# First halves in steps of four chunks, and GpSimd adding to the running total

## The reference

```
def _propagate(all_emb, rows, cols, vals):
    acc = all_emb
    x = all_emb
    for _ in range(N_LAYERS):
        x = jax.ops.segment_sum(vals[:, None] * x[cols], rows, num_segments=N_NODES)
        acc = acc + x
    return acc / (N_LAYERS + 1)
...
users_emb = all_users[users] + _upsample_nearest(mm_users[users])
items_emb = all_items + _upsample_nearest(mm_items)
rating = users_emb @ items_emb.T
rating = rating + bias_user[users] + bias_item.T
return jax.nn.sigmoid(rating)
```

## Time and profile before

| | us |
|---|---|
| median of 3 runs | 5386.34 (5384.41 to 5394.33) |
| the profiled execution | 5386.6 |
| its span | 5384.8 |
| VectorE busy | 4793.2 (89%) |
| TensorE busy | 3361.2 (62%) |
| ScalarE busy | 2443.1 (45%) |
| GpSimd busy | 2415.1 (45%) |

### The profile page before, as it was taken

One profiled execution on the slowest core, in us unless ns is written; L12 is line 12 of the kernel. 1 busy time (PEld: TensorE's weight loads), 2 busy tenths in 40 slices (PEclk: granted clock), 3 DMA queues, 4 the chain that ended last, 5 costly groups with the idle time before them and its releaser, 6 DMA issues.

```text
span 5384.8 us, 195868 instructions
## 1 busy us (share of the span) xinstructions
PE 3361.2 (62%) x71235; PEld 2864.2 (53%) x71473; DVE 4793.2 (89%) x7569; ACT 2443.1 (45%) x4368; POOL 2415.1 (45%) x2161
## 2 busy tenths in 40 slices
PE   5600021111288888777678888867768888867767
PEld 4500011110277777666567777756657777766652
DVE  9989999999999999877799999967789999977778
ACT  0035555553366666500156666620046666640027
POOL 0038763330177777700067777730037777760000
PEclk9955555555699999999999999989989999989989
DMA  9960000300188778799968878889968777879999
GB/s 329 415 260 0 0 0 3 5 0 0 64 248 253 248 246 247 234 321 328 279 213 251 248 256 249 249 276 328 328 191 255 249 245 246 249 241 328 328 281 357
DMA packets 840272, 1191.20 MB, mean 221 GB/s; under 512 B 150792, under 2 KB 667583, under 8 KB 839825
## 3 DMA queue, kind: packets, MB, share of 16 engines
q1 hardware_dynamic: 716032, 816.66, 53.2%
q0 software_dynamic: 123872, 372.78, 18.0%
q10 hardware_dynamic: 304, 1.00, 0.1%
HBM read 638.35 MB, written 551.90 MB: 221 GB/s over the span
## 4 chain that ended last, share of the span: by engine, by line
DVE 28%; DMA 28%; issue 20%; POOL 9%; PE 6%; ACT 5%; SPq 1%; DVEq 1%; POOLq 0%; another core or an unknown queue 0%; ACTq 0%
DMA ring<-posts 15%; DMA posts<-ring 9%; POOL posts L775 9%; DVE store L1064 6%; PE psum L1501 4%; DVE total L861 3%; ACT new L695 3%; DVE store L1042 3%; DVE ring L1271 3%; DVE store L1043 2%; DMA out<-new 2%; DVE new L1243 2%; DVE ring L1256 2%; DVE ring L1295 2%; DMA ring<-lanes_d 1%
## 5 line engine op out<-in xcount | busy, mean ns | idle before, releaser
L775 POOL DMA_INDIRECT posts<-ring x1884 | 1852.6, 983 | 1740.6 <-DVE ring L1256 1154.0
L1477 PE MATMUL psum<-store,ring 128*128 x45216 | 2086.2, 197 | 497.9 <-DVE ring L1271 461.6
L1477 PEld LDWEIGHTS psum<-store,ring 128*128 128x128 bf16 x45216 | 1815.1, 100 | 769.2 <-issue 591.4
L695 ACT ACTIVATE new<-new 128x512 bf16<-128x512 uint8 x1884 | 1067.8, 614 | 0.0
L1271 DVE TENSOR_SCALAR ring<-ring,lane_f 128x1024 bf16<-128x1024 bf16 x1884 | 959.7, 551 | 23.4 <-DMA ring<-lanes_d 22.0
L1295 DVE TENSOR_TENSOR ring<-ring,wide_lane 128x1024 bf16<-128x1024 bf16 x948 | 612.9, 688 | 300.1 <-ACT ring L705 300.1
L1256 DVE TENSOR_TENSOR ring<-new 128x1024 bf16<-128x1024 bf16 x942 | 652.2, 692 | 93.8 <-ACT new L695 63.3
L693 ACT ACTIVATE ring<-new 128x512 bf16<-128x512 bf16 x942 | 585.9, 622 | 310.3 <-DVE new L1243 308.2
L750 POOL TENSOR_TENSOR ring<-store 128x1024 f32<-128x1024 f32 x157 | 369.6, 2354 | 660.6 <-DVE store L982 306.3
L1243 DVE TENSOR_TENSOR new<-psum,vals_m 128x512 f32<-128x512 f32 x942 | 644.1, 684 | 6.1 <-PE psum L1477 4.0
L1501 PE MATMUL psum<-ring 128*128 128x64 bf16 x11520 | 387.4, 193 | 188.7 <-DVE ring L1295 180.9
(11 more groups left out here) (228 smaller groups left out, 2666.1 us busy)
## 6 DMA issues: line engine op xcount, KB each, us to landing
ring<-lanes_d SPq DMA_DIRECT2D x471, 512.0 KB
ring<-posts SPq DMA_DIRECT2D x240, 772.0 KB, 6.7
store<-posts SPq DMA_DIRECT2D x234, 772.0 KB, 6.7
posts<-store SPq DMA_DIRECT2D x2, 30880.0 KB, 166.7
posts<-store SPq DMA_DIRECT2D x2, 30108.0 KB, 128.5
out<-new SPq DMA_DIRECT2D x96, 500.0 KB, 8.4
posts<-ring POOLq DMA_INDIRECT x1884
store<-L_rec_bias_item SPq DMA_DIRECT2D x1, 3125.0 KB, 13.8
```

Source lines behind the costliest of these rows:

```text
L695: last = nc.scalar.activation(digits[s][:, k, :], scaled_byte[s][k], ACT.Copy, scale=scale)
L775: pool.indirect_dma_start(out=posts[:, :], out_offset=bass.IndirectOffsetOnAxis(ap=dring[:, h, c:c + 1], axis=0), in_=msg[:, n, :], in_off ...
L1477: last = pe.matmul(psum[:, d % 4, (n % 2 * BLOCK + b) * F:(n % 2 * BLOCK + b + 1) * F], of, xflat[:, bass.ds(at_d[c] * F + (k * XT + x * F ...
```

## The change

A step of the first half becomes four chunks (157 steps a layer): each of VectorE's and ScalarE's instructions on it is twice as long, and there are half as many. The scale now stands between a step's two one-hots. The message ring is refilled by quarters of four slots, each with a semaphore of its own. GpSimd waits for a message and adds to `s_pace` once for four scatters. The additions to the running total (and the copies in layer 0) move from VectorE to GpSimd, ahead of a layer's scatters; whatever overwrites `new` waits for as many of them as it needs (`TAKEN_FOR`, two, four and seven). So that this works the one-hots, digits and powers move into `new`, the scaled sums into `ring`, and `rest` to another place in `ring`. SyncE's first loads of a layer wait only until the second half before them has been read. `WAYS` is 2, as before, and the loop at the end of the second half (`ADD_BODIES`) is written in another way with the same instructions.

```diff
-        hot = [ring[:, 2048 + s * 1024:3072 + s * 1024].bitcast(BF16).rearrange("p (k e) -> p k e", k=2) for s in range(2)]
+        hot = [new[:, s * WAYS * 1024:(s + 1) * WAYS * 1024].bitcast(BF16).rearrange("p (k e) -> p k e", k=WAYS) for s in range(2)]
...
-        scaled = [new[:, s * 512:(s + 1) * 512] for s in range(2)]
+        dring = ring[:, 10336:10352].bitcast(I32).rearrange("p (h e) -> p h e", h=4)
+        scaled = [ring[:, 2048 + s * 1024:3072 + s * 1024] for s in range(2)]
...
-        digits = [new[:, 1024 + s * 512:1536 + s * 512].bitcast(BF16).rearrange("p (k e) -> p k e", k=2) for s in range(2)]
-        power = [new[:, 2048 + s * 256:2304 + s * 256].bitcast(BF16) for s in range(2)]
+        digits = [new[:, 6144 + s * 1024:7168 + s * 1024].bitcast(BF16).rearrange("p (k e) -> p k e", k=2) for s in range(2)]
+        power = [new[:, 8192 + s * 512:8704 + s * 512].bitcast(BF16) for s in range(2)]
...
-        rest = [ring[:, s * SPLIT * F:(s + 1) * SPLIT * F].rearrange("p (t f) -> p t f", f=F) for s in range(2)]
+        rest = [ring[:, 5200 + s * SPLIT * F:5200 + (s + 1) * SPLIT * F].rearrange("p (t f) -> p t f", f=F) for s in range(2)]
...
-                sp.wait_ge(s_x3, (layer + 1) * SPLITS)
-                def lanes(i, h, n):
-                    for b in range(n // 4):
-                        sp.wait_ge(s_hots, i * 8 + (layer * DUOS + h * 4 + b * 2 + 2))
+                if layer:
+                    sp.wait_ge(s_unit, layer * ITERS + GOTS)
...
-                def refill(i, h, first, n):
+                def refill(i, h, first):
 
                     if layer or not first:
-                        act.wait_ge(s_scat[h], i * 128 + layer * SENT_ROWS[h])
-                    at = bass.ds(i * 16 + h * 8, n)
-                    nc.scalar.activation(dring[:, h, 0:n], dest_m[:, at], ACT.Copy)
-                    nc.scalar.activation(msg_lanes[:, h * 16:h * 16 + 2 * n, :], lanes_m[:, at, :].rearrange("p s (a e) -> p (s a) e", e=2), ACT.Copy)
-
-                def take_apart(i, first, pairs=8):
-                    for d in range(pairs):
+                        act.wait_ge(s_scat[h], i * 64 + layer * SENT_ROWS[h])
+                    at = bass.ds(i * 16 + h * 4, 4)
+                    nc.scalar.activation(dring[:, h, :], dest_m[:, at], ACT.Copy)
+                    nc.scalar.activation(msg_lanes[:, h * 8:h * 8 + 8, :], lanes_m[:, at, :].rearrange("p s (a e) -> p (s a) e", e=2), ACT.Copy)
+
+                def take_apart(i, first, quads=4):
+                    for d in range(quads):
                         s = d % 2
-                        if d % 4 == 0:
-                            refill(i, d // 4, first, min(8, 2 * pairs - 2 * d))
-                        act.wait_ge(s_scaled, i * 8 + (layer * DUOS + d + 5))
-                        nc.scalar.activation(msg_parts[:, 0, 4 * d:4 * d + 4, :], scaled_high[s], ACT.Copy).then_inc(s_high, 1)
+                        refill(i, d, first)
+                        act.wait_ge(s_scaled, i * 4 + (layer * QUADS + d + 5))
+                        nc.scalar.activation(msg_parts[:, 0, 8 * d:8 * d + 8, :], scaled_high[s], ACT.Copy).then_inc(s_high, 1)
...
+                act.wait_ge(s_x3, (layer + 1) * SPLITS)
+                act.wait_ge(s_taken, (layer + 1) * SPLITS)
...
+                if layer:
+                    pool.wait_ge(s_add, layer * ITERS + 2)
+                else:
+                    pool.wait_ge(s_lanesd, 64)
+                    pool.wait_ge(s_decoded, 1)
+                    pool.wait_ge(s_x0, 1)
+                for q in range(SPLITS):
+                    a, b = q * SPLIT, (q + 1) * SPLIT
+                    if layer == 0:
+                        nc.gpsimd.tensor_copy(total3[:, a:b, :], new3[:, a:b, :]).then_inc(s_taken, 1)
+                    else:
+                        nc.gpsimd.tensor_tensor(total3[:, a:b, :], total3[:, a:b, :], new3[:, a:b, :], ALU.add).then_inc(s_taken, 1)
+
                 def scatter(i, chunks):
                     for n in range(chunks):
-                        h, c = n // 8, n % 8
-                        if n % 2 == 0:
-                            pool.wait_ge(s_msg, i * 8 + (layer * DUOS + n // 2 + 1))
-                        pool.sem_inc(s_pace, 1)
+                        h, c = n // 4, n % 4
+                        if c == 0:
+                            pool.wait_ge(s_msg, i * 4 + (layer * QUADS + h + 1))
+                            pool.sem_inc(s_pace, 1)
...
-                pool.wait_ge(s_taken, (layer + 1) * SPLITS)
...
-            def take(layer, q):
-                a, b = q * SPLIT, (q + 1) * SPLIT
-                if layer == 0:
-                    nc.vector.tensor_copy(total3[:, a:b, :], new3[:, a:b, :]).then_inc(s_taken, 1)
-                else:
-                    nc.vector.tensor_tensor(total3[:, a:b, :], total3[:, a:b, :], new3[:, a:b, :], ALU.add).then_inc(s_taken, 1)
...
-                    nc.vector.tensor_tensor(scaled[d % 2].rearrange(by_edge, f=F), psum[:, d % 4, :].rearrange(by_edge, f=F),
-                                            vals_m[:, bass.ds(i * 16 + 2 * at, 2), :].rearrange("p c b -> p (c b)").rearrange("p (e o) -> p e o", o=1).broadcast_to([P, 8, F]),
+                    nc.vector.tensor_tensor(scaled[d % 2].rearrange(by_edge, f=F), psum[:, 2 * d:2 * d + 2, :].rearrange("p a c -> p (a c)").rearrange(by_edge, f=F),
+                                            vals_m[:, bass.ds(i * 16 + 4 * at, 4), :].rearrange("p c b -> p (c b)").rearrange("p (e o) -> p e o", o=1).broadcast_to([P, 16, F]),
                                             ALU.mult).then_inc(s_scaled, 1)
...
-                def send(i, first, pairs=8):
-                    for d in range(pairs):
-                        h, j = d // 4, d % 4
-                        dve.wait_ge(s_sent, i * 8 + (layer * DUOS + d + 1))
-                        if not (first and d < 2):
-                            if first and d == 2:
-                                dve.wait_ge(s_taken, layer * SPLITS + 2)
-                            scale(i, (d + 6) % 8, d - 2)
-                        if j % 2 == 0:
-                            dve.wait_ge(s_idx[j // 2], i * 32 + (layer * HALF_LOADS[j // 2] + h + 1) * 16)
-                        for k in range(2):
-                            last = nc.vector.tensor_scalar(hot[d % 2][:, k, :], idx[j // 2][:, j % 2 * 2 * CHUNK:(j % 2 + 1) * 2 * CHUNK],
-                                                           lane_f[:, k:k + 1], None, ALU.is_equal)
+                def send(i, first, quads=4):
+                    for d in range(quads):
+                        h, b = d // 2, d % 2
+                        dve.wait_ge(s_sent, i * 4 + (layer * QUADS + d + 1))
+                        dve.wait_ge(s_idx[b], i * 32 + (layer * HALF_LOADS[b] + h + 1) * 16)
+                        if first and d < 3:
+                            dve.wait_ge(s_taken, layer * SPLITS + TAKEN_FOR[d])
+                        for k in range(WAYS):
+                            last = nc.vector.tensor_scalar(hot[b][:, k, :], idx[b], lane_f[:, k:k + 1], None, ALU.is_equal)
+                            if k == 0 and not (first and d < 2):
+                                scale(i, (d + 2) % 4, d - 2)
                         last.then_inc(s_hots, 1)
                         if not (first and d < 3):
-                            low_parts(i, (d + 5) % 8, d - 3)
-                        if first and d < SPLITS:
-                            take(layer, d)
+                            low_parts(i, (d + 1) % 4, d - 3)
...
-                        d, c = n // 2, n % 4
+                        d, c = n // 4, n % 4
                         if c == 0:
                             at_d = supers(i, n)
-                        if n % 2 == 0:
-                            pe.wait_ge(s_hots, i * 8 + (layer * DUOS + d + 5))
-                            pe.wait_ge(s_scaled, i * 8 + (layer * DUOS + d + 1))
+                            pe.wait_ge(s_hots, i * 4 + (layer * QUADS + d + 5))
+                            pe.wait_ge(s_scaled, i * 4 + (layer * QUADS + d + 1))```

On VectorE, in the loop over bodies of 16 chunks, this stood for one pair of chunks: L1243 is the scale (`psum` to `new`), L1271 the one-hots, L1252 the mask, L1256 the low parts.

```order
L1243 ISA [waits s_sent]
L1243 TENSOR_TENSOR new<-psum,vals_m 128x512
L1271 TENSOR_SCALAR ring<-ring,lane_f 128x1024 x2
L1251 REGISTER_ALU
L1252 TENSOR_SCALAR new<-ring 128x512 [waits s_high]
L1256 TENSOR_TENSOR ring<-new 128x2x4x128 [waits s_digits,s_power]
```

More of the change, by code:

```diff
@@ L32 @@
 SENTINEL = -float(1 << 100)
-SUPERS = -(-TILES // 2)
+WAYS = 2
+SUPERS = -(-TILES // WAYS)
 BLOCK = 4
@@ L357, in build @@
         s_high = sem("s_high")
-        s_scat = [sem(f"s_scat{h}") for h in range(2)]
+        s_scat = [sem(f"s_scat{h}") for h in range(4)]
         s_got = [sem(f"s_got{s}") for s in range(GOTS)]
@@ L1281, in _ @@
                     send(i, False)
```

(19 more changed lines are left out.)

51 lines of the change are left out of this document (27 added, 24 removed).

## The result

The changed kernel takes 5583.76 us (median of 4 runs, 5571.17 to 5589.76) beside 5388.70 for the kernel before on the same chip: a ratio of 1.0355, 95% interval 1.0341 to 1.0369. The profiled execution took 5585.3 us (span 5583.2).

A forecast was written before the change was run, and what follows sets the result against it. The prediction took GpSimd's row of scatters to bound the first halves. 5386.6 + 240 (scatters held up by VectorE) + 37 (additions) + 3 (start) = 5667 us, range 5410 to 5800.

The forecast's parts named there:

- What bounds the kernel: First halves: GpSimd's scatters, one every 1.265 us, 794 us or 95%, are the bound; VectorE only keeps step.
- What that does to the step: First halves: VectorE slips ahead, waits for ScalarE, and its instructions hold scatters up by chance: 240 us.
- e: Scatters' extra busy time over 0.960 us each, per four chunks: from 0.09 to 0.6 us, bounds 0.09 and 1.0.
- The reasoning by chance and squared lengths: Scatters meeting VectorE instructions by chance lose the sum of squared lengths over twice the period: 1.0 us a step.
- Theory P: Experiments' theory: covered phases of the scatters' beat decide; a free phase cuts excess (busy time over 0.960 each) to 25 us.
- The floor of 794 us plus the few long gaps: First halves: scatter number, form and gaps stay, so each keeps this minimum; no time gained.
- The additions: Layer starts: on GpSimd they delay VectorE's split, 18 us in layers 1 and 2, 10 in layer 0; sum 37.
- The start: Layer starts: earlier lane loads save 4.17 us, the longer way to the first scatter costs more: together 3 us.
- Half in step: Rival, first halves: VectorE finds some phase again, e 0.3, 5526 us; chance 0.22 including a low part that doesn't block.
- The low part doesn't block: Rival, first halves: only one-hots and mask hold scatters up, 5526 us; chance 0.08.
- The scale opens a window: Rival, first halves: 1.14 us free in every step lets four scatters pass without waiting, 5340 us; chance 0.09.
- The semaphore step was in the gap: Rival, between scatters: three of four gaps fall from 0.30 us to nothing, 5237 us; chance 0.03.

The follow-up runs named there:

- b_short_scale: Kernel before, VectorE's scale taking 256 of 512 columns, so half of the messages are old numbers: ratio 1.0211, 5482.2 us.
- a_low2: Changed kernel with a step's low parts made by two instructions of 1024 columns in place of one of 2048: 5573.6 us, ratio 1.0254 to the kernel before.
- a_one_psum: Changed kernel writing only one of two low parts, its other input a cleared PSUM bank: 5540.8 us, ratio 1.0281 to the kernel before.
- a_order: Changed kernel with the scale ahead of both one-hots, as in the kernel before: 5757.6 us, ratio 1.0726 to the kernel before.
- a_fit: Changed kernel, VectorE reordered: one-hot, half scale, one-hot, mask, half low part, half scale, half low part: 5503.4 us, ratio 1.0242 to the kernel before.
- a_pace1: Changed kernel with GpSimd adding to s_pace ahead of every scatter again: 5579.3 us, ratio 1.0273 to the kernel before.
- a_fit_adds: Order of a_fit, with the seven additions on VectorE again, right behind the split: 5450.0 us, ratio 1.0144 to the kernel before.
- b_early: Kernel before with only SyncE's early loads of lane numbers from the change: 5359.1 us, ratio 0.9977.
- a_adds_dve: Changed kernel with the seven copies or additions on VectorE again, right behind the split: 5541.3 us, ratio 1.0193 to the kernel before.
- a_half_psum: Changed kernel with the first digit in PSUM as fp32 and the low part as one instruction per digit: 5630.2 us, ratio 1.0445 to the kernel before.
- b_half_lanes: Kernel before, each load of lane numbers bringing only half its columns, so half the edges get wrong messages: 5349.4 us, ratio 0.9925.

## Why the prediction was right, and where its terms were off

The forecast of 5667 us was on the right side and 83 us too high; the range of 5410 to 5800 holds the time.

**What bounds the kernel** held: GpSimd's row of scatters sets the first half, and halving VectorE's instructions gained nothing by itself. b_short_scale shows the claim at its sharpest: less work on VectorE alone makes the kernel before 2% slower.

**What that does to the step** held in that VectorE ran ahead, waited at the mask and the low part (208 us) and held scatters up, and nearly in the size: e was to go from 0.09 to 0.6 us for every four chunks; measured, 268 us of excess over 471 steps, 0.57. The term is 224 us in place of 240. Not all of it is waiting: every scatter has grown by some 10 ns, 1884 x 0.010 = 19 us, which goes with the additions on GpSimd and was in no term. By the count above, 201 of the 268 us fall on scatters that begin in low parts and 53 on those that begin in one-hots.

The reasoning by chance and squared lengths is not what sets e, though, so that 0.57 came out near 0.6 is in good part luck. By it a_low2 and a_one_psum should have given back much of the term, and a_order little, since its lengths are the same. Instead the waits moved from low parts to one-hots in the first two, and order alone gave 131 to 147 us of excess. What a catch costs depends on where in the scatters' beat of 1.265 us VectorE's instructions stand, and a scatter that escapes one is caught by the next. Theory P had that in it and still gave too little for a_fit (25 against 61). Scatters were to meet VectorE's instructions "where chance has it", "with no step to come back to"; but where VectorE runs without a wait they begin at the same three places of its step each time. That step, 4.20 us, is too short for four scatters (5.06) and longer than three need (3.80), so three scatters lose 0.40 us in each. That a free phase and a VectorE no faster than the beat are both needed fits all runs, but no run has both in steps of four chunks; it is argued, not shown.

**The floor of 794 us plus the few long gaps** is the step that failed: "the few long gaps that no message explains" were to stay, and went. Of the -70 us 14 stops of 3.5 to 6 us are 60, and 15 shorter gaps the rest. Most of the 83 us is this. Bringing the register steps back does not bring the gaps back (a_pace1), and a slower pace of the scatters does not remove them: b_short_scale has an excess of 150 us in all and keeps its gaps, a_fit_adds has 148 and none. What else all kernels with steps of four have is left, for instance the refill by quarters with four semaphores for landings, or one message wait for four scatters. None of it was tried alone; the cause is open.

**The additions** cost on VectorE's split what the earlier trace rows gave: its seven delayed instructions of layer 1 lose (7.32 - 3.1) + 3 x (4.38 - 1.55) + 2 x (4.18 - 1.56) = 18 us, the 18 of the prediction. Off was only the credit: "freed VectorE time in the first steps gives some 3 us a layer back" gave nothing in layers 1 and 2, where the start is later by 18.9 and 18.5, which is 18 + 0.9. In layer 0 10 - 3 + 0.9 = 7.9 was measured to the tenth, but by luck: with the copies beside it VectorE's split takes 28.9 us (1417.42 to 1446.28) in place of 21.6 (1418.05 to 1439.69), so they cost 7.2 and not 10, and the 3 did not come back here either. **The start** held: b_early has the 4.2 us for each layer, and a_adds_dve, with 7 additions of 1.48 us in a row, 428.2 + 10.4 - 4.2 + 5.1 = 439.5 against 440.0 and 441.4.

By terms: 5386.6 + 224 - 70 + 45 = 5585.6, beside 5585.3 measured; on record were 240, 0, 40. Three small errors of the working change little: a held scatter takes longer by what is left of the instruction less some 0.12 us, not by all of it (for that of 3241.09 in the earlier trace rows 0.37 is left, and it takes 0.24 more); the formula gives 0.7 and not 0.8 for the kernel before, by its lengths of 0.48 twice, 0.28 and 0.69; and 0.9 x 471 is 424, not 430.

**The rivals.** "Half in step" had e = 0.3, and 0.57 was measured; VectorE and the scatters did find a phase again, but one of three scatters to a step, which costs more than this rival had. "The low part doesn't block" is refuted for these scatters: 424 of 450 that begin in a low part are slow. The Trainium skill, page "SBUF — State Buffer", section "Who interferes with whom", infers that a tensor_tensor does not stall a DMA issued from GpSimd; 424 of 450 say otherwise here. By a_one_psum and a_half_psum what holds them goes with the second SBUF input: with one input in PSUM the low part lets them pass. The low part on PSUM is also the slower one, 1.22 us for 1024 columns; but the addition to the total, with two SBUF inputs and 1.55 us for 1344, is as slow a column and holds a scatter too, so the pace isn't what decides. "The scale opens a window" is true of the scale (0.970 there), and its place between the one-hots is worth 3 to 4% beside a_order, but of 1884 scatters only 438 begin in the scale and 436 while VectorE is idle, together less than two of four. "The semaphore step was in the gap" is refuted: the 0.30 us are there 627 times.

## What to carry to other kernels

When instructions of one engine can hold up another that sets the time, the first engine's speed is part of the schedule: look whether the two keep step, and what holds the faster one in step, before making its instructions fewer, longer or shorter. Count how many items of the slower engine one cycle of the faster holds: here 2.53 us held two scatters almost without loss, and 4.20 us held three where four were needed. A wait that is removed at one instruction is only gone if the beat as a whole has room; count the waits over all instructions, not over the one that was changed. Of a change with many parts, try the parts alone: here one small part (b_early) was worth 0.2%, and the whole cost 3.5%.

## What the runs showed of the hardware

- A caught scatter nearly always ends 0.81 to 0.87 us behind the instruction that held it (938 of 946 in the changed kernel), whichever that is: one-hot, mask, low part or addition. It can also be held near its end: in a_one_psum 206 scatters that began 0.14 to 0.46 us ahead of a one-hot end 0.12 us behind it. A one-hot that begins 0.10 us behind a scatter's start does not hold it.
- In the kernel before GpSimd stops for 3.5 to 6 us at fixed counts, ahead of the 114th, 226th, 338th, 450th and 562nd scatter of layer 0, so every 112, with nothing that the profile shows to wait for. The places are the same in b_half_lanes and b_short_scale, at another pace; half the bytes of lane numbers make the stops shorter. One of each:

```profile
3194.50 1.03 POOL L775 DMA_INDIRECT posts<-ring  x1 [2.68 <-DVE ring L1256]
```

```profile
3260.57 0.96 POOL L775 DMA_INDIRECT posts<-ring  x1 [3.24 <-issue]
```

  (b_half_lanes, which the view puts down to a message, and b_short_scale.) Their cause stays open.
- Unhindered scatters take 0.970 to 0.971 us on average (those that began with VectorE idle) in all eight kernels with the additions on GpSimd, and 0.959 to 0.963 in the six without. Why is open.
